# Attention and mixture-of-experts kernel: the router's steps spread over ticks, the second norm's rows and a gate made on ScalarE

## Chip, cores and metric

One core of a Trainium2 chip. The metric is device time in microseconds for one execution of the whole kernel; the number of a kernel is the median of its runs.

## What is computed

For x of shape (8, 512, 128), float32:

```python
x = x + attention(layernorm(x))     # 16 heads of 8 channels, causal, W_qkv, W_proj, biases
x = x + experts(layernorm(x))
# experts(xf), 8 experts, hidden width 512:
logits = xf @ Wg                    # (4096, 8)
top_vals, top_idx = top_k(logits, 2)
gate = softmax(top_vals)
comb = einsum('tke,tk->te', one_hot(top_idx), gate) * alpha
hdn = layernorm(xf) * ln_w[e] + ln_b[e]
y_e = gelu(hdn @ fc1_w[e] + fc1_b[e]) @ fc2_w[e] + fc2_b[e]
out = sum over e of y_e * comb[:, e]
```

The router works on the rows that the second layer norm makes (z below), and the experts' own layer norm on z is folded into a second root (`rstd_two[:, 0]`).

## The kernel before

The program is written without a scheduler: every engine walks one list, `schedule`, and takes from it the stages that it has a handler for, in the list's order. Semaphores join the engines. So what stands ahead of a stage in the list stands ahead of it in an engine's queue.

The attention stage is cut into 8 batches x 4 groups of 4 heads, and a group into 11 units (`UNIT`): four of 512 columns, four of 384, and three with more than one head. Group after group gives 352 units. The list runs in ticks n = 0, 1, 2, ...; in each tick stand `pass1` of unit n, `pass2` of unit n - 24, and, seven ticks later and for some units only, one row of `pv`. A batch is 44 ticks.

- `pass1` (TensorE L648, with a causal matmul L644) makes logits in one of six PSUM slots; VectorE takes the row maximum (L940 for one head, L934 for more), which frees the slot.
- `pass2` (TensorE L665) makes the transposed logits less the maximum in a slot of the same ring; ScalarE takes the exponential (L811), GpSimd cuts the diagonal block (L1252), and TensorE multiplies with v (`pv`, L680).
- `max_parts` (GpSimd L1264, L1267) and `maxT` (TensorE L687, VectorE L948) carry the maxima of a group to the second pass. `pv_out` (ScalarE L816) copies a group's result, which SyncE stores.

Everything else is put at a tick by tables, relative to a batch's first tick. `FRONT`, `APPLY`, `SPLIT` and the two `HALF` tables do so for the next batch's layer norm (`ln_stats` L870, `ln_agg` L877 with the add of epsilon L882, GpSimd's root L1163, `ln_apply` in quarters L893), the projections q, k and v, and the three-part splits of q and k (ScalarE L789, GpSimd L1244), which SyncE stacks. `BACK` holds the way from a batch's attention result to the residual (`o_load` to `proj`, VectorE L953, L958, L964, TensorE L695). `ROUTE` and `DISPATCH` hold the router:

| stage | engine, lines | what it does |
|---|---|---|
| r_stats, r_agg | VectorE L870, L877, L888, L889 | mean and variance, two variances |
| r_root | GpSimd L1184 | the two roots |
| r_z | VectorE L893, L976 | z = (x - mean) * root for four tiles of 128 rows, and a ratio |
| zT, gate | TensorE L602, L707; ScalarE L769; VectorE L980 | transpose and logits of 8 experts |
| r_top | VectorE L987 to L1005 | two largest, their indices, their difference, `pick`, `sel` |
| r_exp | GpSimd L1191 | the second gate as a power of e |
| r_copy | ScalarE L828 | second copy of z |
| r_comb | VectorE L1010 to L1020 | gates, alpha, written into z |
| rank | TensorE L715 to L721; VectorE L1026 to L1034 | place of each token in its expert's list |
| dispatch | GpSimd L1235, eight for a batch | z rows written to their places in DRAM |

One PSUM bank, `misc`, serves all small products; each is read at the start of the next tick, or ahead of the next product (`read_misc`). Within VectorE's steps `link` makes every instruction wait for the one before it:

```python
def link(ins):
    ins.then_inc(s_ln, 1)
    chain[0] += 1
    dve.wait_ge(s_ln, chain[0])
```

After tick 358 come the steps of the first table (`t_count` to `t_row`, VectorE), which lists the expert tiles of the first six batches; tiles 0 and 1 are loaded at tick 366. Steps of batches 6 and 7 that are left over when the attention ends stand between the expert tiles by the dictionary `LATE`. There follow 39 expert tiles (`turn_z`, `fc1`, `fc2`, `turn_y`; TensorE L731, L739, L748, L756, ScalarE L834, L841, VectorE L1120, L1126), the first 17 from the first table, the rest after batch 7 is dispatched. At the end y is read back and summed.

## Time and profile before

| | us |
|---|---|
| median of three runs (lowest to highest) | 540.84 (540.76 to 541.0) |
| span of the profiled execution | 560.3 |
| TensorE, VectorE, ScalarE, GpSimd busy | 473.9, 373.1, 322.9, 366.1 |
| first routing (z of batch 0) to last unit's pv | 112 to 367 |
| expert tiles, first to last of TensorE | 369 to 537 |

The time is measured without the profiler; the profiled execution is a separate one, and of it the span alone, from first to last instruction, is known. It is 19.5 us longer than the median. Differences are read in the trace and set against the median.

### The profile page before, as it was taken

What the parts mean: (1) busy time and instruction counts of PE and PEld (TensorE: products, weight loads), DVE (VectorE), ACT (ScalarE), POOL (GpSimd) and SP (SyncE); (2) the same over time, 40 slices, a digit from 0 to 9 for tenths busy, and PEclk for the clock granted to TensorE, in tenths of its full rate; (3) what the DMA queues carried; (4) which work ended last, traced back from release to release, by engine and by line L of the source; (5) the groups of instructions that cost most, each with busy time, mean ns of one, the idle gap of its engine ahead of it and who ended that gap; (6) DMA issues with size and microseconds to landing.
All of it is one profiled execution on the core that took longest, in us unless ns stands there. A gap on an engine that the chain in (4) does not pass through costs nothing.

```text
span 560.3 us, 11807 instructions
## 1 busy us (share of the span) xinstructions
PE 473.9 (85%) x3296; PEld 277.1 (49%) x3296; DVE 373.1 (67%) x1316; ACT 322.9 (58%) x661; POOL 366.1 (65%) x712
## 2 busy tenths in 40 slices
PE   3379999999999998998898988786992999999930
PEld 1134443543443453443444443364981888888920
DVE  4588878889889889889889997741543521222226
ACT  2137786776676776676676666752550555565610
POOL 5956676586986986987887876955556444445520
PEclk9589999999999999999999999897996899999985
DMA  2323133134233234234224212276642685666439
GB/s 62 93 57 105 65 93 109 58 105 118 68 101 117 78 87 129 73 91 130 75 66 130 71 40 79 79 236 213 219 159 86 213 264 180 216 194 187 154 129 328
DMA packets 52726, 70.83 MB, mean 126 GB/s; under 512 B 11063, under 2 KB 38430, under 8 KB 52662
## 3 DMA queue, kind: packets, MB, share of 16 engines
q1 hardware_dynamic: 47478, 59.19, 34.7%
q0 software_dynamic: 4320, 8.53, 4.5%
q10 hardware_dynamic: 864, 2.36, 1.2%
q8 instruction: 27, 0.44, 0.3%
q14 instruction: 37, 0.30, 0.2%
HBM read 36.49 MB, written 20.94 MB: 102 GB/s over the span
## 4 chain that ended last, share of the span: by engine, by line
PE 51%; DVE 17%; issue 8%; POOL 6%; SPq 5%; DMA 4%; another core or an unknown queue 4%; ACT 3%; ACTq 0%; DVEq 0%; POOLq 0%
PE acc_bank L748 10%; PE slots L739 10%; PE slots L648 7%; PE acc_bank L680 7%; PE slots L665 5%; SPq L496 4%; DVE masked L940 3%; PE misc L616 3%; POOL z_dram L1235 2%; DVE z L893 2%; DVE row_max L934 2%; POOL probs L1252 2%; DMA y_in<-y_dram 2%; PE slots L644 2%
## 5 line engine op out<-in xcount | busy, mean ns | idle before, releaser
L811 ACT ACTIVATE probs<-slots 128x512 f32<-128x512 f32 (+1 forms) x352 | 185.6, 562 | 86.0 <-PE slots L665 79.2
L940 DVE CUSTOM_DVE_ANT_0 masked<-slots,causal_row 128x512 bf16<-128x512 f32 (+1 forms) x256 | 148.9, 614 | 20.8 <-PE slots L648 20.7
L648 PE MATMUL slots<-stack_k,stack_q 125*128 125x256 bf16 (+3 forms) x512 | 128.5, 307 | 19.4 <-DVE row_max L940 7.5
L1252 POOL TENSOR_SCALAR_AFFINE_SELECT probs<-probs 128x128 f32<-128x128 f32 (+2 forms) x352 | 116.1, 350 | 41.3 <-ACT probs L811 37.4
L665 PE MATMUL slots<-stack_q,stack_k 128*128 128x256 bf16 (+3 forms) x512 | 125.6, 301 | 2.9 <-DVE row_max L934 1.5
L1282 POOL DMA_INDIRECT y_dram<-y,z_in x71 | 69.7, 982 | 73.4 <-DVE y L1126 56.8
L841 ACT ACTIVATE hidden<-slots,w_in 128x256 f32<-128x256 f32 (+1 forms) x156 | 63.1, 455 | 82.6 <-PE acc_bank L748 29.2
L680 PE MATMUL acc_bank<-probs,v 128*32 128x512 f32 (+3 forms) x1024 | 95.6, 447 | 3.4 <-POOL probs L1252 2.7
L648 PEld LDWEIGHTS slots<-stack_k,stack_q 125*128 125x128 bf16 x512 | 48.3, 99 | 95.4 <-DVE row_max L940 49.7
L1235 POOL DMA_INDIRECT z_dram<-z,pos x64 | 63.6, 994 | 32.1 <-DVE pos L1034 17.7
L748 PE MATMUL acc_bank<-hidden,w_in 128*128 128x256 f32 (+1 forms) x312 | 73.0, 376 | 7.8 <-issue 4.0
L934 DVE TENSOR_REDUCE row_max<-slots 128x2 f32<-128x512 f32 (+1 forms) x96 | 63.7, 689 | 14.0 <-PE slots L648 13.2
L739 PE MATMUL slots<-hdnT,w_in 128*128 128x256 f32 (+1 forms) x312 | 71.1, 372 | 1.4 <-ACT hdnT L834 0.7
L748 PEld LDWEIGHTS acc_bank<-hidden,w_in 128*128 128x128 f32 x312 | 54.6, 196 | 15.9 <-ACT hidden L841 5.8
L739 PEld LDWEIGHTS slots<-hdnT,w_in 128*128 128x128 f32 x312 | 57.4, 197 | 9.8 <-issue 1.9
L665 PEld LDWEIGHTS slots<-stack_q,stack_k 128*128 128x128 bf16 x512 | 46.0, 98 | 25.7 <-issue 6.5
L1126 DVE TENSOR_TENSOR y<-slots,z_in 128x256 f32<-128x256 f32 (+1 forms) x39 | 15.6, 400 | 54.4 <-issue 33.5
L1120 DVE TENSOR_SCALAR yT<-acc_bank,w_in 128x256 f32<-128x256 f32 (+1 forms) x39 | 17.8, 457 | 49.8 <-PE acc_bank L748 37.4
L680 PEld LDWEIGHTS acc_bank<-probs,v 128*32 128x32 f32 x1024 | 20.4, 108 | 36.9 <-issue 17.2
L644 PE MATMUL slots<-causal,ident_b 128*128 128x256 bf16 (+1 forms) x96 | 30.6, 319 | 0.2 <-DVE row_max L940 0.2
L834 ACT ACTIVATE hdnT<-slots,w_in 128x256 f32<-128x256 f32 (+1 forms) x39 | 21.2, 543 | 2.8 <-PE slots L731 2.8
L756 PE MATMUL slots<-ident,yT 128*128 128x128 f32 x71 | 14.6, 280 | 8.0 <-issue 7.6
(168 smaller groups left out, 523.1 us busy)
## 6 DMA issues: line engine op xcount, KB each, us to landing
w_in<-in_wpack SPq DMA_DIRECT2D x39, 516.0 KB
o_dram<-oT SPq DMA_DIRECT2D x32, 256.0 KB, 2.3
stack_k<-parts SPq DMA_DIRECT2D x95, 64.0 KB
stack_q<-parts SPq DMA_DIRECT2D x93, 64.0 KB
z_in<-z_dram SPq DMA_DIRECT2D x32, 132.0 KB
xt<-in_x SPq DMA_DIRECT2D x8, 256.0 KB, 3.7
onT<-o_dram SPq DMA_DIRECT2D x8, 256.0 KB
o_inv<-inv_dram SPq DMA_DIRECT2D x8, 256.0 KB
```

The lines of the kernel that those rows point to most:

```text
L648: mm = pe.matmul(cols[:, i, :], q[0:K1, hh, blk * P:blk * P + P], k[0:K1, hh, 0:w], start=len(heads) == 1, stop=True, skip_group_check=True)
L665: mm = pe.matmul(cols[:, i, :], k[0:K2, hh, blk * P:blk * P + P], q[0:K2, hh, blk * P:T], start=True, stop=True)
L680: mm = pe.matmul(acc_bank[32 * h:32 * h + 32, row * P:T], v1[:, b % 2, row, HPG * hg + h, :], p, start=(row == 0), stop=(row == PV_ORDER[- ...
L739: pe.matmul(half(slots[:, k, :], i), weights(i)[:, k * P:k * P + P], hdnT[:, i % 2, 0:rows_of(i)], start=True, stop=True)\
L748: mm = pe.matmul(half(acc_bank[:, :], i), weights(i)[:, F + k * C:F + k * C + C], hidden[:, i % 2, k, 0:rows_of(i)], start=k == 0, stop=k ...
L811: act.activation(probs_of(n), columns(n, slot), ACT.Exp, scale=SCALE).then_inc(s_exp, 1)
L841: act.activation(hidden[:, i % 2, k, 0:rows_of(i)], half(slots[:, k, :], i), ACT.Gelu_apprx_tanh, bias=aux(i, 2 + k))\
L934: dve.tensor_reduce(largest, columns(n, slot), AX.X, ALU.max).then_inc(s_max, 1)
L940: dve.tensor_tensor_reduce(out=masked[:, n % MASKED, 0:w], in0=slots[:, slot, 0:w], in1=causal_row[:, T - w:T], scale=1.0, scalar=NEG, op0 ...
L1235: pool.indirect_dma_start(out=z_dram[:, :], out_offset=bass.IndirectOffsetOnAxis(ap=pos[:, b % 2, i:i + 1], axis=0), in_=z[:, b % 2, j, n, ...
L1252: pool.affine_select(out=diag, in_=diag, compare_op=ALU.is_ge, fill=0.0, base=0, pattern=[[0, len(heads)], [1, P]], channel_multiplier=-1) ...
L1282: pool.indirect_dma_start(out=y_dram[:, :], out_offset=bass.IndirectOffsetOnAxis(ap=z_in[:, i % Z_RING, n, ID:ID + 1].bitcast(U32), axis=0 ...
```

## The change

- The linked steps of `r_top`, `r_comb` and `rank` become steps of their own, one or two per tick (`STEPS_OF` lists them). `link` gives way to `step`, which counts, and `stepped`, which waits ahead of the instruction that needs the result. `r_stats` comes in two halves and `r_agg` in two steps.
- For batches 0 to 6 z is made by ScalarE as x * root + shift, a tile of 128 rows (a quarter) per tick. VectorE makes `shift` = -mean * root in a new step `r_shift`. In batch 6 the four quarters stand together. Batch 7 keeps VectorE.
- The second gate is `exp(diff)` on ScalarE for batches 0 to 6. Batch 7 keeps GpSimd.
- Between the request of a root and its use lie more ticks: `ln_agg` at 2, `ln_var` at 3, `APPLY` at 7, 8, 8, 9 for 6; `r_shift` at 111. xnT, q, k and the splits follow two ticks later, the dispatches seven. `base` gets two buffers.

```diff
-FRONT = {"ln_stats": 1, "ln_agg": 3, "xnT": 8, "q": 10, "k": 15, "v": 31}
-APPLY = (6, 6, 6, 6)
-SPLIT = ((11, 12, 16, 18), (17, 18, 26, 29))
+FRONT = {"ln_stats": 1, "ln_agg": 2, "ln_var": 3, "xnT": 10, "q": 12, "k": 17, "v": 31}
+APPLY = (7, 8, 8, 9)
+SPLIT = ((13, 14, 18, 20), (19, 20, 28, 31))
...
-ROUTE = (("r_stats", 102), ("r_agg", 105), ("r_root", 105), ("r_z", 109), ("zT", 112), ("gate", 114), ("r_top", 118),
-         ("r_exp", 119), ("r_copy", 114), ("r_comb", 122), ("rank", 124))
-DISPATCH, DISPATCH_STEP = 123, 3
+ROUTE = (("r_stats", 102, 0), ("r_stats", 103, 1), ("r_agg", 104), ("r_var", 105), ("r_root", 105), ("r_shift", 111),
+         ("r_z", 112, 0), ("r_z", 113, 1), ("r_z", 114, 2), ("r_z", 115, 3), ("zT", 117), ("gate", 119), ("r_copy", 118),
+         ("r_max", 120), ("r_index", 121), ("r_diff", 122), ("r_scaled", 123), ("r_exp", 124), ("r_pick", 124),
+         ("r_sel", 125), ("rank", 126), ("g_sum", 126), ("g_first", 127), ("g_second", 128), ("p_mask", 128),
+         ("g_alpha", 129), ("p_sum", 129), ("g_store", 130), ("p_store", 130))
...
+LAST_ROUTE = (("r_stats", 94), ("r_agg", 95), ("r_root", 97), ("r_shift", 101), ("r_z", 101), ("zT", 109), ("gate", 111), ("r_copy", 111),
+              ("r_top", 115), ("r_exp", 116), ("r_comb", 116), ("rank", 118), ("places", 119))
+DISPATCH, DISPATCH_STEP, LAST_EARLY_STEP = 130, 3, 2
...
+            def make_z(b, n):
+                if b == B - 1:
+                    return
+                if n == 0:
+                    wait(act, s_shift, b + 1)
+                    wait(act, s_disp[b % 2], 16 * 2 * NT * (b // 2))
+                ins = act.activation(z[:, b % 2, 0, n, 0:C], xt[:, NT * b + n, :], ACT.Identity,
+                                     scale=rstd_two[:, 0, n:n + 1], bias=shift[:, n:n + 1])
+                if n == NT - 1:
+                    ins.then_inc(s_z, 1)
+
+            def second_gate(b):
+                if b == B - 1:
+                    return
+                wait(act, s_diff, b + 1)
+                act.activation(second[:, :], diff[:, :], ACT.Exp).then_inc(s_second, 1)
...
+            def step(ins):
+
+                ins.then_inc(s_ln, 1)
+                chain[0] += 1
+
+            def stepped():
+
+                dve.wait_ge(s_ln, chain[0])
...
-            def make_z(b):
+            def find_shift(b):
                 wait(dve, s_rtwo, b + 1)
-                wait(dve, s_disp[b % 2], 16 * 2 * NT * (b // 2))
-                normalise(z[:, b % 2, 0, :, 0:C], xt[:, NT * b:NT * b + NT, :], rstd_two[:, 0, :]).then_inc(s_z, 1)
                 dve.tensor_tensor(ratio[:, :], var_two[:, 0, :], rstd_two[:, 0, :], ALU.mult).then_inc(s_ratio, 1)
+                wait(dve, s_z, b)
+                dve.scalar_tensor_tensor(shift[:, :], mean_var[:, :, 0], -1.0, rstd_two[:, 0, :], ALU.mult, ALU.mult)\
+                   .then_inc(s_shift, 1)
...
-                link(last)
+                step(last)
+
+            def find_index(b):
+                stepped()
                 for n in range(NT):
                     last = dve.max_index(top_at[:, n, :], top[:, n, :], gate_in[:, n, :])
-                link(last)
+                step(last)
```

The order of instructions shows three places. In its rows `stats`, `probs` and the like are the tiles of the text above, and `probs<-slots` is the second pass's exponential.

VectorE, routing of batch 3: from the steps of `r_comb` to the last step of `rank`. Before:

```order
L1010 TENSOR_SCALAR denom<-second 128x4
L1011 RECIPROCAL gates<-denom 128x4
L1012 TENSOR_TENSOR gates<-gates,second 128x4
L1015 TENSOR_TENSOR by_alpha<-pick,alpha_s 128x64
L1018 TENSOR_REDUCE alpha_of<-by_alpha 128x8
L1019 COPY z<-token_ids 128x8
L1020 TENSOR_TENSOR z<-alpha_of,gates 128x8
L940 ISA masked,row_max<-slots,causal_row 128x512
```

The change:

```order
L1073 TENSOR_TENSOR sel<-pick 128x32
L983 ISA masked,row_max<-slots,causal_row 128x384
L983 ISA row_max 128x1
L1077 TENSOR_SCALAR denom<-second 128x4
L1105 TENSOR_TENSOR place_of<-misc,base 128x32
L1107 TENSOR_TENSOR base<-misc,base 128x8
L983 ISA masked,row_max<-slots,causal_row 128x384
L983 ISA row_max 128x1
L1081 RECIPROCAL gates<-denom 128x4
L991 COPY max_rows<-misc 48x128
```

The gates' steps stood in one piece and now have units of the first pass between them; one unit lies between the selection and the reading of `rank`.

ScalarE, the end of the attention with batch 6. Before:

```order
L811 ACTIVATE probs<-slots 128x512 x7
L811 ACTIVATE probs<-slots 128x384 x4
L816 ACTIVATE oT<-acc_bank 128x512
L811 ACTIVATE probs<-slots 128x512
L769 ACTIVATE zT<-misc 128x512
L811 ACTIVATE probs<-slots 128x512 x2
L828 ACTIVATE z<-z 128x4x128
L816 ACTIVATE oT<-acc_bank 128x512
```

The change:

```order
L828 ACTIVATE probs<-slots 128x512 x4
L849 ACTIVATE z<-xt,shift,rstd_two 128x128 x4
L828 ACTIVATE probs<-slots 128x512 x3
L828 ACTIVATE probs<-slots 128x384 x4
L833 ACTIVATE oT<-acc_bank 128x512
L828 ACTIVATE probs<-slots 128x512
L786 ACTIVATE zT<-misc 128x512
L828 ACTIVATE probs<-slots 128x512 x2
L862 ACTIVATE z<-z 128x4x128
L858 ACTIVATE second<-diff 128x4
```

The four quarters stand among the seven exponentials, ten exponentials come behind them, and the gate's exponential stands ahead of the last `oT`.

GpSimd, from the tenth tick or so of a period on. Before:

```order
L1244 TENSOR_TENSOR qk<-qk,parts 128x512
L1235 DMA z_dram<-z,pos 35072x132
L1252 AFFINE_SELECT probs<-probs 128x128 x5
L1184 TENSOR_TENSOR rstd_two<-var_two,minus_half 128x8
L1252 AFFINE_SELECT probs<-probs 128x128
L1244 TENSOR_TENSOR parts<-qk,parts 128x512
L1244 TENSOR_TENSOR qk<-qk,parts 128x512
```

The change:

```order
L1327 DMA z_dram<-z,pos 35072x132
L1344 AFFINE_SELECT probs<-probs 128x128
L1336 TENSOR_TENSOR qk<-qk,parts 128x512
L1344 AFFINE_SELECT probs<-probs 128x128 x2
L1327 DMA z_dram<-z,pos 35072x132
L1344 AFFINE_SELECT probs<-probs 128x128
L1275 TENSOR_TENSOR rstd_two<-var_two,minus_half 128x8
L1344 AFFINE_SELECT probs<-probs 128x128 x2
L1327 DMA z_dram<-z,pos 35072x132
L1344 AFFINE_SELECT probs<-probs 128x128
L1336 TENSOR_TENSOR parts<-qk,parts 128x512
L1336 TENSOR_TENSOR qk<-qk,parts 128x512
```

Between the first split and the last two there was one dispatch; now there are two, and one more just ahead of them.

## Rows read from the trace of the kernel before

**Rows 1.** The page: span, and busy time of each engine (share, instructions)
```profile
span 560.3 us, 11807 instructions
...
PE 473.9 (85%) x3296; PEld 277.1 (49%) x3296; DVE 373.1 (67%) x1316; ACT 322.9 (58%) x661; POOL 366.1 (65%) x712
```

**Rows 2.** Windows of one period: busy us (instructions) of each engine, TensorE's granted clock, DMA
```profile
213.91:217.83 3.92, 3.08 (x25) 0.87 (x25) 3.82 (x19) 2.24 (x5) 1.38 (x3) 1.00 0.46 143
...
221.74:225.66 3.92, 3.52 (x24) 1.10 (x21) 3.88 (x19) 2.47 (x6) 3.09 (x9) 1.00 0.17 50
225.66:229.58 3.92, 2.89 (x30) 1.50 (x29) 3.07 (x12) 1.54 (x4) 3.52 (x9) 1.00 0.31 100
...
241.32:245.24 3.92, 3.53 (x26) 1.40 (x23) 3.92 (x10) 3.04 (x7) 3.77 (x9) 1.00 0.50 151
...
253.07:256.99 3.92, 3.27 (x29) 1.19 (x27) 3.75 (x14) 2.36 (x5) 3.22 (x9) 1.00 0.47 145
sum 43.08, PE 39.77 PEld 18.04 DVE 38.48 ACT 30.04 POOL 34.97; mean PE 3.62 PEld 1.64 DVE 3.50 ACT 2.73 POOL 3.18
```

**Rows 3.** ScalarE in order of time, start and length: the copies of xnT
```profile
62.77 0.60 ACT L769 ACTIVATE xnT<-misc 128x512 f32<-128x512 f32 x1 [0.45 <-PE misc L602]
...
99.69 0.60 ACT L769 ACTIVATE xnT<-misc 128x512 f32<-128x512 f32 x1 [0.45 <-PE misc L602]
...
143.12 0.60 ACT L769 ACTIVATE xnT<-misc 128x512 f32<-128x512 f32 x1 [1.85 <-PE misc L602]
```

**Rows 4.** VectorE in order of time, the same period
```profile
227.29 1.15 DVE L893 TENSOR_SCALAR xn<-xt,mean_var,rstd 128x128 f32<-128x128 f32 x4 [0.85 <-POOL rstd L1163]
...
241.90 2.07 DVE L893 TENSOR_SCALAR z<-xt,mean_var,rstd_two 128x128 f32<-128x128 f32 x4
...
252.99 0.19 DVE L1005 TENSOR_TENSOR sel<-pick 128x32 bf16<-128x32 f32 x1
...
256.35 0.22 DVE L1015 TENSOR_TENSOR by_alpha<-pick,alpha_s 128x64 f32<-128x64 f32 x1
256.60 0.22 DVE L1018 TENSOR_REDUCE alpha_of<-by_alpha 128x8 f32<-128x64 f32 x1
```

**Rows 5.** ScalarE: one group by form; then in order of time, the same period
```profile
L834 ACT ACTIVATE hdnT<-slots,w_in 128x128 f32<-128x128 f32 x7 | 3.3, 469 | 0.0
...
243.93 0.60 ACT L811 ACTIVATE probs<-slots 128x512 f32<-128x512 f32 x1 [0.63 <-PE slots L665]
244.78 0.60 ACT L769 ACTIVATE zT<-misc 128x512 f32<-128x512 f32 x1 [0.25 <-PE misc L602]
245.56 1.16 ACT L811 ACTIVATE probs<-slots 128x512 f32<-128x512 f32 x2 [0.18 <-PE slots L665]
```

**Rows 6.** GpSimd's groups in the period; then GpSimd and TensorE in order of time
```profile
L1235 POOL DMA_INDIRECT z_dram<-z,pos x8 | 8.0, 1000 | 4.2 <-DVE pos L1034 2.5 <-issue 1.1 <-POOL max_parts L1267 0.6
...
L1252 POOL TENSOR_SCALAR_AFFINE_SELECT probs<-probs 128x512 f32<-128x512 f32 x4 | 2.6, 640 | 0.2
L1244 POOL TENSOR_TENSOR qk<-qk,parts 128x512 f32<-128x512 f32 x2 | 2.3, 1152 | 0.0
...
245.67 1.40 POOL L1252 TENSOR_SCALAR_AFFINE_SELECT probs<-probs 128x512 f32<-128x512 f32 x4
...
250.18 0.43 PE L680 MATMUL acc_bank<-probs,v 128*32 128x128 f32 x8
```

**Rows 7.** The tail in order of time: ScalarE, VectorE, GpSimd, TensorE
```profile
354.02 4.47 ACT L811 ACTIVATE probs<-slots 128x512 f32<-128x512 f32 x9
...
362.97 1.08 ACT L811 ACTIVATE probs<-slots 128x512 f32<-128x512 f32 x2
...
359.77 1.44 DVE L893 TENSOR_SCALAR z<-xt,mean_var,rstd_two 128x128 f32<-128x128 f32 x4
...
356.82 1.68 POOL L1184 TENSOR_TENSOR rstd_two<-var_two,minus_half 128x8 f32<-128x8 f32 x1
...
365.76 1.50 PE L680 MATMUL acc_bank<-probs,v 128*32 128x384 f32 x24
```

More of the change, by code:

```diff
@@ L111, in build @@
         n = NG * UNITS * b
-        for name, m in ROUTE:
-            at(n + m - SOONER.get((b, name), 0), name, b)
+        if b < EARLY_BATCHES:
+            for name, m, *part in ROUTE:
+                at(n + m, name, b, *part)
+        else:
+            for name, m in LAST_ROUTE:
+                for step, *part in STEPS_OF.get(name, ((name,),)):
+                    at(n + m, step, b, *part)
         for i in range(2 * NT):
-            at(n + DISPATCH + DISPATCH_STEP * i - SOONER.get((b, "dispatch"), 0), "dispatch", b, i)
+            step = LAST_EARLY_STEP if b == EARLY_BATCHES - 1 else DISPATCH_STEP
+            at(n + DISPATCH + step * i, "dispatch", b, i)
         if b == EARLY_BATCHES - 1:
```

140 lines of the change are left out of this document (90 added, 50 removed).

## The prediction, made before the changed kernel was run

> **What bounds the kernel now.** The page comes first: over the whole span TensorE is busy 85%, VectorE 67%, GpSimd 65%, ScalarE 58% [rows 1]. That is an average of two stages. The change moves work in the first, attention and routing up to about 368 us, so I read that one. The median of the runs is 540.84 us, 19.5 us under the span of the profiled execution (560.3 us); I work out differences on the trace and take them off the median unchanged, since the stage runs at the full granted clock (1.00, the 2.4 GHz level) [rows 2].
>
> Second view: one period of 44 ticks, from the end of one batch's gates to the next, cut into eleven pieces [rows 2]. TensorE is busy 39.77 of 43.08 us, VectorE 38.48. The six pieces that are not shown have TensorE busy for (nearly) all of their time. The five shown have nearly all its idle time: 0.84, 0.40, 1.03, 0.39 and 0.65 us, which is 3.31 together and equals 43.08 - 39.77. So neither engine bounds the period; they take turns. Third view: without routing a period lasts 99.69 - 62.77 = 36.9 us, the first one with routing 143.12 - 99.69 = 43.4 us [rows 3]. Routing and the work that comes with it add 6.5 us, while the idle time above shows that half of this is not TensorE's own work. **The floor of a period is about 39.8 us**, unless TensorE's own work changes, and it does not.
>
> Fourth view: VectorE in order of time at those pieces [rows 4]. The normalisation waits 0.85 us for GpSimd's root and then takes 1.15 us in one stretch; z takes 2.07 us in one stretch; the selection at 252.99 ends a run of linked instructions that stand behind one another, and the gates' steps at 256.35 and 256.60 are part of a second such run. TensorE holds at most a few units ahead, as there are six PSUM slots for both passes, so each such stretch turns into TensorE's idle time.
>
> **What is taken off VectorE.** (1) z, 2.07 us for a batch [rows 4], goes to ScalarE for seven of eight batches. One instruction for the shift comes in; its nearest row is the 0.22 us of a step on 64 columns [rows 4], and I take 0.17. (2) The linked steps. A step behind a link starts 0.25 us after a predecessor that is 0.22 long (256.35 and 256.60) [rows 4]; an unlinked one can start inside the end of the last. About 14 links in a batch, each worth between 0.03 (the gap) and 0.15 us (gap and overlap), give 0.4 to 2.1 us; I take 1.2, as several of the steps now stand next to each other all the same. (3) The wait of 0.85 us for the root [rows 4]: four ticks and more now lie between the request and the first normalised quarter. Together VectorE loses 2.07 - 0.17 + 1.2 + 0.85, about 4 us of 43.
>
> **What of it reaches the end.** Only TensorE's idle time can. From routing: 0.84 (gates and places), 0.39 (z), 0.65 (maximum to selection) [rows 2]. I take 0.65, 0.35 and 0.40, not all, since the same steps remain and the ticks with reduces stay full; 1.4 us for a batch, six batches (0 to 5): 8.4 us. From the layer norm: 0.40 and 1.03 [rows 2]; I take 0.2 and 0.6, because the last quarter of xn now stands one tick before TensorE's transpose where all of it stood two before, in ticks where VectorE's reduces leave no room. 0.8 us in the five loaded periods (batches 3 to 7): 4.0 us. **Gain 12.4 us.** Bounds: nothing, if the spread steps only wait elsewhere, and 6 x 1.88 + 5 x 1.43 = 18.4 us, if all five pieces close.
>
> **What is added.** (a) TensorE's rank now comes one tick after VectorE's selection (before: six ticks, [rows 4] has the selection at 252.99). A unit on VectorE and the selection must fit into a tick that has two short matmuls and a row of pv: I charge 0.2 us, between 0 and 0.8, six times: 1.2 us.
>
> (b) ScalarE. Four quarters at 0.469 us, the row of the same function with scale and bias from tiles and 128 columns [rows 5], 1.9 us a batch. They lie in ticks that have an exponential of 0.60 us each, and there ScalarE was idle 0.63 + 0.25 + 0.18 us [rows 5]. But the copy of zT (0.60) moves out of this stretch, so 1.9 stands against 1.7: cost 0, up to 0.5 a batch if the exponentials come late enough for TensorE to see it; TensorE's second pass may run three units ahead, which covers that much. The gate's exponential is one more small ScalarE instruction in place of GpSimd's 1.0 us. For VectorE's own rate there is a row as well: four took 1.44 us where little else ran [rows 7], so ScalarE is the slower engine for this work. The Trainium skill, ScalarE: Activation LUTs, section "Rules for kernel authors", says to put add and multiply on VectorE, not on ScalarE, as VectorE is faster for them. By that rule the move would be a loss of about 0.4 us a batch; by the rows it is a gain as long as VectorE ends last there. The trace agrees with the rule on speed, and not on which engine should have the work. In the period z took 2.07 us, 0.6 more than in the tail [rows 4, 7]. The Trainium skill, SBUF — State Buffer, section "Who interferes with whom", says that VectorE in a two-port mode and GpSimd fully block one another and that ScalarE waits for neither. By it the 0.6 us would go away with the move; if it were only handed to VectorE's next instruction, my gain of z would be 1.44 and not 2.07. No row of this trace decides that.
>
> (c) GpSimd, the part that I trust least. The dispatches of a batch move by 7 ticks, its splits by 2. From the 10th to the 23rd tick of a period its queue now has four dispatches, three splits, the two-norm root and 14 selects. Before it was two dispatches (the first at the ninth tick). A select takes up to 0.64 us, a dispatch 1.0, a split 1.15, the root 1.68 [rows 6, 7]. Before, the select that the fourth row of pv needs ended at 245.67 + 0.64 = 246.3 us, and TensorE used it at 250.18: 3.9 us to spare [rows 6]. Off come two dispatches (2.0 plus their gaps, 2.3), about 1.0 as twenty ticks each become 0.05 us shorter, and 0.7 because the queue no longer starts on a dispatch one tick earlier. That leaves nothing. I charge 0.5 us of TensorE waiting for GpSimd's selects, between 0 and 1.5, in the four periods with dispatches, splits and root together: 2.0 us.
>
> (d) The tail, batch 6. Its z stands in ScalarE's queue between two exponentials of the second pass. VectorE finds the shift only behind the first table, about where z began before, 359.77 [rows 7]. ScalarE reached this place in its queue before at 354.02 + 4 x 0.53 = 356.1 (three exponentials of 512 columns take 1.6) and went on with exponentials to 358.5. Now it **stands until about 360.1**, then makes four quarters (4 x 0.469 less some overlap, 1.7), then has ten exponentials, oT and zT (twelve at the 4.47 / 9 of the row's run): 361.8 + 6.0 = 367.8, where the last exponential ended at 364.05 before [rows 7]. TensorE had slack behind that: pv, the gate and three more rows of pv ran to 367.3 [rows 7]. With the gate (about 1 us) behind zT at 366.8 and 1.5 us of pv it ends near 369.3: 2.0 us later. GpSimd's root of batch 6 (356.8, [rows 7]) has two more dispatches ahead of it, but idle time further up, so some 1 us later and not last. I charge 2.2 us, between 1 and 4. Everything after (the store of the last heads, the weights of the third tile) follows that end, so it passes in full. The gate's exponential of batch 6 stands ahead of oT's last copy and waits for VectorE; this is in the 4. The stage of the experts keeps its order, cost 0.
>
> **Sum:** 12.4 - 1.2 - 0 - 2.0 - 2.2 = 7.0 us; 540.84 - 7.0 = **533.8 us** (1.3% faster). A measurement can tell some 0.2%, 1.1 us, from no change.
>
> **Rivals.**
>
> *All of TensorE's idle time goes.* For: VectorE has 4 us less to do in a period that misses its floor by 3.3; the period without routing shows what TensorE can do. Against: the new short distances in (a) and to xn. 18.4 - 1 = 17.4 us, 523.4 us; this case covers 523 to 529. Chance 0.17.
>
> *ScalarE takes VectorE's place.* For: 1.9 us more in ticks with 1.06 us idle. The rule on add and multiply above would make it so. Against: three units of lead. Then some 0.9 us a batch come back as waits for the exponentials, 5.4 us, and half of the layer norm's 4.0 goes: 7.0 - 7.4, about no change. It covers 538.5 to 542. Chance 0.12.
>
> *GpSimd becomes the bound, and the kernel is slower.* The place is TensorE's pv at ticks 23 to 30 of periods 3 to 6. The price: two dispatches and the late splits in full, some 3 us in each of four periods (12), with the tail at 4 and 0.5 for each rank (3), against 12.4: 6.6 us slower, 547.4 us. It decides from a wait of 12.4 - 1.2 - 2.2 = 9.0, a quarter of which is 2.25 us a period, on. For: GpSimd's queue is full there by my count. Against: 3.9 us to spare before. Chance 0.13.
>
> *The change does not do what it says.* The order of instructions shows z and the steps moved, so nothing is left for this case.
>
> **How the numbers follow.** My own case, 529 to 538.5 us, has 0.58. Below 525 lie some 0.07, a third of the first rival and a little; above 541 some 0.13. The range is 525 to 541. Faster by over 0.2%: 0.58 + 0.17 + 0.05 of the second rival, 0.80. Within it 0.07, slower 0.13.
>
> **What would show it.** Right: a period near 41.3 us between two transposes of xn, no wait of VectorE for the root, TensorE waiting less than 2 us a period, z quarters near 0.47 us on ScalarE, and in the tail a ScalarE stall of some 4 us before the first z quarter of batch 6. Wrong: periods still at 43 us; waits of pv for selects of over 2 us a period; no stall in the tail, which would put the time 2 us lower; or the stage of the experts, from the first expert tile on, changing its length.

## The result, and the profile after

| | before | after |
|---|---|---|
| median of four runs each, us | 540.92 (540.76 to 541.39) | 554.86 (552.77 to 555.19) |
| span of the profiled execution | 560.3 | 553.1 (its own time 554.9) |
| first matmul of an expert tile | 368.56 | 382.53 |

The changed kernel is **slower by 2.44%**, ratio 1.0244, 95% interval 1.0223 to 1.0264, or 13.9 us. The forecast was 533.8 us, with 525 to 541 as its range: wrong in sign and outside the range.

The two spans cannot be compared with each other. The profiled execution of before has a longer stage of the experts than its timed runs have. The kernel before was timed again on four chips: 540 us on one and 562 to 564 on three, and executions like the latter are 20 us longer behind the first expert tile alone. Ahead of it, two profiles of before agree within 0.7 us (368.56 here, 369.28 below). Of the runs further down, one of e4 (796 us), one of e6 (2499 us) and two of e8 (568 us) fell in a slow state and are left out of the ratios. So I measure each kernel at **the turn**, the start of TensorE's first transpose of an expert tile. First before, then after:

```profile
368.56 0.42 PE L731 MATMUL slots<-ident,z_in 128*128 128x128 f32 x2
```

```profile
382.53 0.42 PE L748 MATMUL slots<-ident,z_in 128*128 128x128 f32 x2
```

The turn is 14.0 us later, which is the whole 13.9 us of the times. The busy time of the engines on the page of after hardly tells of it: VectorE has 15 us less than in [rows 1], ScalarE 6 more.

```profile
span 553.1 us, 11783 instructions
...
PE 467.6 (85%) x3264; PEld 274.7 (50%) x3296; DVE 357.8 (65%) x1296; ACT 329.2 (60%) x696; POOL 361.3 (65%) x705
```

ScalarE of after in order of time, the copies of xnT, against [rows 3]:

```profile
64.80 0.60 ACT L786 ACTIVATE xnT<-misc 128x512 f32<-128x512 f32 x1 [0.28 <-PE misc L619]
...
104.09 0.60 ACT L786 ACTIVATE xnT<-misc 128x512 f32<-128x512 f32 x1 [0.28 <-PE misc L619]
...
148.69 0.60 ACT L786 ACTIVATE xnT<-misc 128x512 f32<-128x512 f32 x1 [0.99 <-PE misc L619]
...
193.53 0.60 ACT L786 ACTIVATE xnT<-misc 128x512 f32<-128x512 f32 x1 [0.60 <-PE misc L619]
...
238.35 0.60 ACT L786 ACTIVATE xnT<-misc 128x512 f32<-128x512 f32 x1 [0.60 <-PE misc L619]
```

A period without routing takes 39.3 us where it took 36.9; nothing of the router runs there, so these 2.4 us are a cost of the front. A full period takes 44.8 us where [rows 2] have 43.08. The window of that full period of after:

```profile
193.53:238.35 44.82, 39.60 (x313) 18.24 (x316) 36.83 (x140) 30.92 (x63) 34.13 (x76) 1.00 0.32 92
```

TensorE's work is as forecast (39.60 after 39.77), VectorE has 1.65 us less, and TensorE is idle for 5.2 us instead of 3.3. What it waited for in that period, from the summary of its waits:

```profile
PE slots L665 <- DVE row_max L983: 1.8, 2, 1.1
PE misc L619 <- DVE xn L936: 0.8, 1, 0.8
PE misc L704 <- ACT qk L795: 0.8, 1, 0.8
PE misc L724 <- ACT v L840: 0.7, 1, 0.7
PE misc L732 <- DVE sel L1073: 0.5, 1, 0.5
PE misc L712 <- ACT qk L795: 0.3, 1, 0.3
```

Three of the six are waits for **the one `misc` bank** behind ScalarE's reading of a projection: maxT (L704) behind k, the gate (L724) behind v, proj (L712) behind q. Over the same kind of period the trace of before has none of them. Each wait also stops VectorE, whose queue has the reader of the product ahead of further maxima. VectorE of after, the gate's reading:

```profile
217.89 0.19 DVE L1033 COPY gate_in<-misc 128x32 f32<-128x32 f32 x1 [2.11 <-PE misc L724]
```

The largest wait, for `row_max`, has this behind it. VectorE, GpSimd and TensorE in order of time:

```profile
206.90 0.69 DVE L983 CUSTOM_DVE_ANT_0 masked<-slots,causal_row 128x512 bf16<-128x512 f32 x1
...
207.51 1.73 DVE L1017 TENSOR_TENSOR ratio<-var_two,rstd_two 128x4 f32<-128x4 f32 x1
209.16 0.42 DVE L1019 SCALAR_TENSOR_TENSOR shift<-mean_var,rstd_two 128x4 f32<-128x4 f32 x1
...
206.93 1.17 POOL L1336 TENSOR_TENSOR parts<-qk,parts 128x512 bf16<-128x512 f32 x1
208.05 1.15 POOL L1336 TENSOR_TENSOR qk<-qk,parts 128x512 f32<-128x512 f32 x1
...
210.25 0.34 PE L665 MATMUL slots<-stack_k,stack_q 125*128 125x384 bf16 x1 [1.14 <-DVE row_max L983]
```

The ratio, four columns wide, takes 1.73 us and ends with GpSimd's pair of splits (208.05 + 1.15 = 209.20).

### The profile page after: what moved, and what is told of

It is laid out like the page before. It is cut to its first block, busy times and chain, and to the rows that moved or that the text cites. A ratio compares the mean times of both kernels' runs of the same rounds, so it can differ in the third digit from the quotient of the medians.

```text
span 553.1 us, 11783 instructions
## 1 busy us (share of the span) xinstructions
PE 467.6 (85%) x3264; PEld 274.7 (50%) x3296; DVE 357.8 (65%) x1296; ACT 329.2 (60%) x696; POOL 361.3 (65%) x705
## 4 chain that ended last, share of the span: by engine, by line
PE 51%; DVE 13%; issue 11%; ACT 9%; POOL 6%; DMA 6%; SPq 3%; ACTq 0%; DVEq 0%; POOLq 0%
PE acc_bank L765 10%; PE slots L756 10%; PE acc_bank L697 7%; PE slots L665 7%; PE slots L682 5%; ACT probs L828 3%; PE misc L633 3%; POOL probs L1344 3%; DVE row_max L977 2%; DMA y_in<-y_dram 2%; DVE masked L983 2%; SPq L513 2%; DVE xn L936 2%; ACT qk L795 2%; POOL z_dram L1327 1%
## 5 line engine op out<-in xcount | busy, mean ns | idle before, releaser
L828 ACT ACTIVATE probs<-slots 128x512 f32<-128x512 f32 (+1 forms) x352 | 183.5, 562 | 84.5 <-PE slots L682 76.9
L983 DVE CUSTOM_DVE_ANT_0 masked<-slots,causal_row 128x512 bf16<-128x512 f32 (+1 forms) x256 | 150.9, 613 | 23.1 <-PE slots L665 22.0
L1344 POOL TENSOR_SCALAR_AFFINE_SELECT probs<-probs 128x128 f32<-128x128 f32 (+2 forms) x352 | 118.3, 350 | 71.7 <-ACT probs L828 66.9
L682 PE MATMUL slots<-stack_q,stack_k 128*128 128x384 bf16 (+3 forms) x507 | 124.8, 302 | 3.0 <-DMA stack_q<-max_rows 2.6
L697 PE MATMUL acc_bank<-probs,v 128*32 128x512 f32 (+3 forms) x1024 | 97.4, 454 | 4.5 <-POOL probs L1344 4.5
L1327 POOL DMA_INDIRECT z_dram<-z,pos x64 | 63.9, 998 | 22.3 <-issue 12.4
L756 PE MATMUL slots<-hdnT,w_in 128*128 128x256 f32 (+1 forms) x312 | 68.5, 362 | 1.4 <-ACT hdnT L868 0.7
L765 PE MATMUL acc_bank<-hidden,w_in 128*128 128x256 f32 (+1 forms) x312 | 68.1, 361 | 0.0
L756 PEld LDWEIGHTS slots<-hdnT,w_in 128*128 128x128 f32 x312 | 55.3, 190 | 8.7 <-issue 1.9
L983 DVE DVE_READ_ACCUMULATOR2_ANT row_max<- 128x1 f32 x256 | 20.8, 81 | 0.0
L661 PE MATMUL slots<-causal,ident_b 128*128 128x256 bf16 (+1 forms) x69 | 20.3, 295 | 0.3 <-DVE row_max L983 0.2
```

The costliest lines, as they stand in the source:

```text
L682: mm = pe.matmul(cols[:, i, :], k[0:K2, hh, blk * P:blk * P + P], q[0:K2, hh, blk * P:T], start=True, stop=True)
L697: mm = pe.matmul(acc_bank[32 * h:32 * h + 32, row * P:T], v1[:, b % 2, row, HPG * hg + h, :], p, start=(row == 0), stop=(row == PV_ORDER[- ...
L756: pe.matmul(half(slots[:, k, :], i), weights(i)[:, k * P:k * P + P], hdnT[:, i % 2, 0:rows_of(i)], start=True, stop=True)\
L765: mm = pe.matmul(half(acc_bank[:, :], i), weights(i)[:, F + k * C:F + k * C + C], hidden[:, i % 2, k, 0:rows_of(i)], start=k == 0, stop=k ...
L828: act.activation(probs_of(n), columns(n, slot), ACT.Exp, scale=SCALE).then_inc(s_exp, 1)
L983: dve.tensor_tensor_reduce(out=masked[:, n % MASKED, 0:w], in0=slots[:, slot, 0:w], in1=causal_row[:, T - w:T], scale=1.0, scalar=NEG, op0 ...
```

## Experiments

| kernel | time, us | before, same chip | ratio (interval) | late period | turn |
|---|---|---|---|---|---|
| e0 | 562.64 | 561.74 | one run | 43.1 | 369.28 |
| e1 | 562.59 | 561.74 | 1.0021 (0.9997, 1.0045) | 43.8 | 374.26 |
| e2 | 579.35 | 561.74 | 1.0289 (1.0254, 1.0324) | 45.7 | 385.16 |
| e3 | 572.90 | 561.74 | 1.0176 (1.0142, 1.0209) | 44.8 | 382.35 |
| e4 | 554.49 | 540.23 | 1.0268 (1.0247, 1.0288) | 44.8 | 381.65 |
| e5 | 552.58 | 540.23 | 1.0234 (1.0217, 1.0251) | 44.6 | 380.03 |
| e6 | 540.58 | 540.23 | 1.0003 (0.9989, 1.0018) | 42.5 | 367.85 |
| e7 | 545.40 | 540.23 | 1.0094 (1.0076, 1.0112) | 43.8 | 373.51 |
| e8 | 564.68 | 562.18 | 1.0012 (0.9984, 1.0040) | 44.9 | 374.56 |
| e9 | 573.23 | 562.18 | 1.0184 (1.0150, 1.0217) | 44.7 | 382.08 |
| e10 | 556.24 | 562.18 | 0.9884 (0.9844, 0.9924) | 42.6 | 367.34 |
| e11 | 560.82 | 562.18 | 0.9977 (0.9951, 1.0003) | 43.1 | 372.80 |
| e12 | 583.73 | 564.18 | 1.0348 (1.0300, 1.0397) | 47.5 | 390.21 |
| e13 | 567.60 | 564.18 | 1.0058 (1.0028, 1.0088) | 43.7 | 376.22 |
| e14 | 570.43 | 564.18 | 1.0104 (1.0052, 1.0156) | 44.6 | 379.76 |
| e15 | 558.17 | 564.18 | 0.9909 (0.9874, 0.9943) | 42.6 | 366.79 |
| e16 | 554.75 | 540.62 | 1.0259 (1.0241, 1.0277) | 44.8 | 381.79 |
| e17 | 546.26 | 540.62 | 1.0107 (1.0089, 1.0125) | 43.1 | 372.99 |

Late period: from the sixth copy of xnT to the seventh (186.21 to 229.29 in before). Where before takes 540 us, time less turn is 171.7 to 172.4 us for before and 171.9 to 173.3 for the others, so the ratio and the turn say the same. Where before takes 562 to 564, time less turn is 193.4 in e0, 193.5 in e12 and 188.0 to 194.2 in the others, so a turn later by 5 us can be hidden there (e1). **I compare turns and periods.** Two profiles of one kernel differ by 0.7 us (before, e0) and 0.9 us (after, e4) at the turn, and by under 0.05 us in a late period; a difference below these says nothing. The 0.9 us lie in the tail, where TensorE's granted clock falls now and then. It falls in single periods of other runs too, and a turn then holds more than the edit: I give the clock where it does.

### Which part costs: the front's tables or the rest

e0 is before again. e1 is the change with the tables of before for the next batch's front (the two stacking tables, `FIRST_HALF` and `SECOND_HALF`, go with them; `ln_agg` and `ln_var` stay at 2 and 3); e2 is before with the new tables.

```diff
-FRONT = {"ln_stats": 1, "ln_agg": 2, "ln_var": 3, "xnT": 10, "q": 12, "k": 17, "v": 31}
-APPLY = (7, 8, 8, 9)
-SPLIT = ((13, 14, 18, 20), (19, 20, 28, 31))
+FRONT = {"ln_stats": 1, "ln_agg": 2, "ln_var": 3, "xnT": 8, "q": 10, "k": 15, "v": 31}
+APPLY = (6, 6, 6, 6)
+SPLIT = ((11, 12, 16, 18), (17, 18, 26, 29))
...
```

> The kernel before, unchanged, for a second profile. The first one's span is 19.5 us longer than its timed runs, while the changed kernel's profiled execution took as long as its timed runs. Theory A (the first profile fell on a disturbed execution, in the stage of the experts): span near 539 us, turn of the first expert tile still at 368 to 369 us, the waits of 6 and 12 us at 376 and 419 us gone. Rival (profiling itself lengthens this kernel): span near 560 us again.

> The change, with the layer norm's, projections' and splits' ticks of before (xnT 8, q 10, k 15, quarters of xn at tick 6, splits as before). Theory 1 (the two ticks' shift puts q one tick ahead of proj, k in one tick with maxT, and the last quarter of xn next to its transpose, all on the one misc bank, so TensorE waits for ScalarE's copy and VectorE): 540 to 545 us, the wait for the copy of qk gone. Theory 2 (ScalarE's z, and VectorE's ratio and shift caught behind GpSimd, cost the time; the shift of the front costs only what is seen before the first routing, 3.7 us): 550 to 552 us.

> The kernel before with nothing but the change's ticks for xnT, q, k, quarters of xn and splits. Theory 1 (shift of the front): 548 us or more, the copy of qk waited for in every period. Theory 2: 543 to 545 us.

e0's profiled execution took 562.64 us on a chip where the timed runs of before took 560.04 to 563.64, so profiling by itself does not lengthen the kernel there.

Measured from the side of the change, the tables cost 382.5 - 374.3 = 8.3 us; put on before, they cost 385.2 - 368.6 = 16.6 us. Of the 16.6, about 1.9 are TensorE's clock: in e2's period without routing (41.49 us long) it is granted 0.96 on average and 0.50 from 98 to 100 us, behind a wait of 2.25 us, and TensorE is busy 38.00 us where before has 36.13. So the front's tables are 8.3 us of the 14.0. The rest of the change costs the other 5.7 us on the old tables, and gives 2.6 us back on the new ones, or some 0.7 without the fall of the clock: the parts collide with each other, and their costs do not add.

### The tail: who makes z of batch 6

e3 is the change with `make_z` on VectorE for batch 6 too (`if b >= 6` for `if b == B - 1`). e4 is the change again, on the chip that e5 to e7 used.

> The change, but z of batch 6 is made by VectorE. Theory 3 (ScalarE's queue stands for the shift of batch 6 behind the table, which costs the tail 2 to 4 us): 551 to 553 us and the first expert tile 2 to 4 us earlier than 382.5. Rival (the tail is set by pv, the gate and GpSimd, and ScalarE has slack there): 554 to 555 us.

> The change, unchanged, beside the kernel before on the same chip as the other runs of this call. If only the chip makes before take 541 or 562 us, the difference stays 13 to 15 us and the first expert tile turns near 382.5 us.

In e3 the turn is at 382.35 after 382.53, no difference. ScalarE of after does stand for the shift, though for a shorter time than the forecast had:

```profile
370.61 1.65 ACT L849 ACTIVATE z<-xt,shift,rstd_two 128x128 f32<-128x128 f32 x4 [2.48 <-DVE shift L1019]
```

Without it the tail is no shorter. From the last `proj` ahead of it to the turn there are 368.56 - 348.78 = 19.8 us in before, 382.53 - 358.51 = 24.0 in after. TensorE's waits from 340 us to the turn name others, first before and then after:

```profile
PE acc_bank L680 <- POOL probs L1252: 2.7, 2, 1.8
PE misc L715 <- DVE sel L1005: 1.1, 1, 1.1
```

```profile
PE acc_bank L697 <- POOL probs L1344: 4.3, 2, 2.4
PE misc L732 <- DVE sel L1073: 2.5, 2, 1.2
```

Together 3.0 us more, of which 1.3 us (one of the two waits for `sel`) lie ahead of the last `proj`. GpSimd of after has eight dispatches from 356.16 to 373.86 with the selects between them. That they cost the 1.6 us of the first row is a reading; no run moved them. The larger part of the 4.2 us is TensorE's clock, as the windows from the last `proj` to the turn show, before and then after:

```profile
348.78:368.56 19.78, 15.07 (x142) 7.27 (x138) 12.54 (x60) 12.13 (x25) 15.16 (x31) 0.91 0.34 112
```

```profile
358.51:382.53 24.02, 17.51 (x140) 7.75 (x138) 11.34 (x60) 13.56 (x30) 18.17 (x35) 0.79 0.31 98
```

TensorE is busy 2.4 us longer for the same work, at a mean granted clock of 0.79 after 0.91; its idle time is 1.8 us more. The clock differs between executions of one kernel: in e4 the same stretch takes 21.9 us at 0.84, so of the 4.2 us 2.1 are gone there.

### The shared bank: k, q and v, one tick apart

```diff
-FRONT = {... "q": 12, "k": 17, "v": 31}
+FRONT = {... "q": 12, "k": 16, "v": 31}   e5
+FRONT = {... "q": 11, "k": 16, "v": 31}   e9
+FRONT = {... "q": 12, "k": 17, "v": 32}   e13
```

> The change with k at tick 16, no longer in one tick with maxT (17). Theory 1a (one bank with two products in one tick is what costs): TensorE's wait for the copy of qk ahead of max_parts (0.8 us a period) goes, seven periods, 5 us or so faster than the change. Theory 1b (the late xn and q beside proj cost it, maxT is hidden): within 1.5 us of the change.

> The change with q at 11 and k at 16: q is no longer one tick ahead of proj (13), k no longer in maxT's tick. Theory 1d: 4 to 6 us faster than the change, 2 to 4 more than k alone gave. Theory 1c: no more than 1 us beyond k alone, which was 1.9 us faster than the change.

> The change with v at 32 alone, out of the gate's tick. With the front's ticks of before this took the period from 43.8 to 42.5 us. Theory 1a: the same here, 1 us or more a period, the first expert tile 5 us or more earlier than 382. Rival (with the late front another wait takes its place): 1 to 2 us in all.

k: the turn comes 2.5 us earlier than in the change (1.6 than in e4), a late period takes 0.25 us less, and maxT's wait over 60 to 340 us falls from 4.7 to 2.7. With q moved as well it is 382.08; what k gave is gone again. The trace of e9 shows where: over the same stretch the wait of proj for q is gone (1.7 us), but q now waits for the copy of xnT one tick ahead of it (1.5 us in all), and the wait for `row_max` grows from 7.3 to 8.8, as the ratio takes 2.04 us in place of 1.72. v: **6.3 us** of 14.0 for one number, 1.17 us a period. That is rather too low, since in e13's period without routing the clock falls to 0.50 from 98 to 100 us, behind a wait of 2.13 us, and the period takes 41.1 us where after has 39.3. The gate's product is at tick 119, and 119 - 2 x 44 = 31, v's own tick; before it was at 114, which is 26. In the period of e13 the row of L724 is gone and the others stand nearly as they were.

### The front back, and v out of the gate's tick

e6 is e1 with v at 32. e7 is e1 with VectorE making z in its quarters, v at 31. e10 is e6 with VectorE making z of batch 6. e15 is e10 with `r_shift` at 109 and the layer norm's first three steps one tick earlier.

> The front's ticks of before, and v at tick 32, one behind the gate (119 is 31 of its period) where both stood in one tick. Theory 1a: the 0.69 us wait of the gate for ScalarE's copy of v goes, and VectorE's 2.1 us idle time with it; six batches, 4 us less than the run with the front's ticks of before alone, so 2 to 4 us faster than before. Rival (VectorE and GpSimd behind it set the period anyway): same as that run, within 1.5 us of before.

> The front's ticks of before, and z on VectorE for all batches, still a quarter per tick; the second gate stays on ScalarE. Theory 4 (ScalarE's z is worth its 2 us of VectorE a batch): slower than the run with the front's ticks of before alone by 4 us or more, less some 3 us for the tail, so 1 to 5 us slower than before. Rival 5 (VectorE had that room once the steps are spread, and ScalarE's late copies of v and zT hold TensorE up): 3 us or more faster than before.

> The front's ticks of before, v at 32, and z of batch 6 on VectorE: the parts of the change that should pay, without the three that should not. The tail gives back 2 to 3 us: 2 to 3 us faster than before. Rival: with batch 6 on VectorE the table's chain and z hold the end up in another way, same as before.

> The front's ticks of before with the layer norm's statistics one tick earlier (0, 1, 2), v at 32, ratio and shift at 109, z of batch 6 on VectorE. Against the run with v and z of batch 6 alone: VectorE's 0.98 us for the root and 1.2 us of ratio go, 0.5 to 1 us a period; 5 us or more faster than before, the first expert tile at 362 to 365 us. Rival (TensorE at its floor of 39.8 and GpSimd now set the period): no more than 1 us beyond that run.

e6 against e1: 374.26 to 367.85, 6.4 us, the same as e13 shows from the other side. With it turn and time are those of before: up to the last copy of xnT e6 is 2.9 us ahead, and the tail takes 2.2 us of it back. Its period and TensorE's waits in it:

```profile
184.18:226.72 42.54, 39.01 (x314) 18.25 (x317) 36.31 (x140) 31.05 (x63) 34.19 (x76) 1.00 0.33 97
```

```profile
PE slots L665 <- DVE row_max L983: 1.0, 2, 0.7
PE misc L619 <- DVE max_rows L991: 0.7, 1, 0.7
PE acc_bank L697 <- POOL probs L1344: 0.5, 1, 0.5
PE misc L704 <- POOL max_parts L1359: 0.5, 1, 0.5
PE misc L732 <- DVE sel L1073: 0.5, 1, 0.5
```

So the spread steps, ScalarE's z and v one tick later are together worth 0.5 us a period (43.1 to 42.5), once nothing collides; the forecast had 1.4 for the routing and 0.8 for the layer norm.

e7 against e1 (both with v at 31) is the comparison for z: 373.51 and 374.26, no difference, both with periods of 43.8 us. VectorE has 37.07 us of work in a period with z and 36.11 without. Neither bounds it: **which engine makes z does not matter here**, while v's tick stands in the way. With v at 32 this pair was not run. e10 and e15 take less time than before where they ran (0.9884 and 0.9909), but only 1.2 and 1.8 us of that is at the turn against 368.56; the other 4 to 5 us lie in the stage of the experts, on chips where that stage takes 20 us longer. Their periods are 0.5 us shorter than those of before, as e6's are, and e6 gained nothing in its time. No run shows what they do on the chip where before takes 540 us. e15 was to come to 362 to 365 us and came to 366.79. Its ratio was to get shorter and takes 2.50 us, where e10's takes 1.22; its late period is 42.58 us all the same, after 42.57. So a longer hold of the ratio need not reach the end.

### What is late by itself: the splits, the quarters of xn

e8 is e6 with the change's ticks for the splits and their stackings; xnT, q, k and xn's quarters stay at the ticks of before. e11 is e6 with `APPLY = (6, 6, 7, 7)`, so xn's last quarter stands one tick ahead of TensorE's transpose, as in the change.

> The run with the front's ticks of before and v at 32, but with the change's later ticks for the splits and their stacking (q and k stay at 10 and 15). Theory 1c (the late splits are the costly part of the front: they meet ScalarE's z quarters, VectorE's ratio behind GpSimd, and SyncE's stores of the maxima queue behind the late stackings): 4 us or more over that run. Theory 1d (the products on the one bank are the costly part): within 2 us of it.

> The run with the front's ticks of before and v at 32, but the last two quarters of xn at tick 7, one tick ahead of the transpose at 8, as the change has it (9 and 10). If this short distance is what TensorE's waits for xn in the change come from (0.5 to 1.2 us a period): 2 to 5 us over that run. If the spreading pays for it (VectorE's wait for the root falls from 0.99 us): within 1 us.

e11: the turn is 4.95 us later, TensorE waits 1.4 us for xn in its late period (first row below), which e6 does not have. About 1 us of the 4.95 is clock: the period ahead of it takes 44.05 us at 0.97 where the late one takes 43.09 at 1.00. e8: 6.7 us later, with the ratio at 3.03 us, VectorE and GpSimd in order of time:

```profile
PE misc L619 <- DVE xn L936: 1.4, 1, 1.4
```

```profile
201.47 3.03 DVE L1017 TENSOR_TENSOR ratio<-var_two,rstd_two 128x4 f32<-128x4 f32 x1
...
202.21 1.16 POOL L1336 TENSOR_TENSOR parts<-qk,parts 128x512 bf16<-128x512 f32 x1
203.32 1.15 POOL L1336 TENSOR_TENSOR qk<-qk,parts 128x512 f32<-128x512 f32 x1
```

201.47 + 3.03 = 204.50, and 203.32 + 1.15 = 204.47: whenever it starts, it ends with the pair. That became the theory of the last runs. e8 holds the comparison within itself. Two of its periods, 44.94 and 44.90 us, have the ratio at 3.03 us, and in both the clock is granted 0.96. In the next period the ratio gets through ahead of the pair, and the period is as long as e6's (42.71), with the splits just as late:

```profile
246.40 0.18 DVE L1017 TENSOR_TENSOR ratio<-var_two,rstd_two 128x4 f32<-128x4 f32 x1
```

```profile
232.55:275.29 42.74, 39.01 (x318) 18.34 (x317) 35.31 (x140) 31.20 (x63) 34.34 (x76) 1.00 0.33 97
```

### The ratio and GpSimd's splits

```diff
-         ... ("r_root", 105), ("r_shift", 111),
+         ... ("r_root", 105), ("r_shift", 109),   e12; e14 with k 16, v 32, VectorE's z in batch 6
+         ... ("r_root", 105), ("r_shift", 112),   e16; e17 with k 16, v 32
```

> The change with the step that makes ratio and shift at tick 109 for 111, ahead of GpSimd's two splits. Theory 1c (ratio, with two inputs in SBUF, stands until GpSimd's splits are through: 1.7 us in the change): ratio takes 0.2 us, TensorE's wait of 1.1 us for the maximum goes, the period falls by about 1 us in four periods, the first expert tile turns 3 to 5 us earlier. Rival (VectorE stands there for something else, or the time goes to the next wait): less than 1 us.

> The change with its late front kept, but k at 16, v at 32, ratio and shift at 109, z of batch 6 on VectorE. If these four and not the late front as such are the loss, all of it goes: 540 us on a chip where before takes 540 (within 3 us of before), the first expert tile near 369. If what is left of the late front (xn next to its transpose, q next to proj) counts: 3 to 7 us slower than before.

> The change, but with r_shift at 112 for 111 (the step stands one unit later in VectorE's queue, still ahead of the first quarter of z). Theory A, the ratio of L1017 is held while GpSimd's two splits run side by side with it: in the change it starts at 207.51, 0.58 us into the pair (206.93 to 209.20), and ends with the pair; put two ticks earlier it started ahead of the pair, took 2.94 us and still ended with it. One tick later it starts at or just behind the end of the pair, so it takes under 0.5 us, TensorE's wait for row_max falls by 0.8 to 1.2 us in each period with routing and splits (four of them), and the expert tiles' first turn moves from 382.5 to 377.5 to 379.5 us. Price: ScalarE gets the shift 0.3 to 0.6 us later, and the transpose of z may wait for it by as much. Rival B, the ratio is slow by itself in this part of the tick (its operands, or VectorE's state behind the masked reduction): it takes 1.3 to 1.7 us again, wherever it stands, and the turn stays within 0.8 us of 382.5.

> The change with three things mended and the front still late: v at 32, k at 16, r_shift at 112. v alone brought the turn from 382.5 to 376.2, k alone to 380.0. If the three collisions are separate and theory A of the run before holds, the turn comes to 376.2 - 2.5 - 4 = about 370 to 372 us, one to three above the kernel before (368.6), and what is left is the last quarter of xn one tick ahead of its transpose and the tail; the time is within 0.6% of the kernel before. Rival: the late front costs by the late splits as such, by what stands behind them in GpSimd's queue and not through the ratio; then the turn stays at 374 us or later, as with the splits alone moved late (374.56).

e12 was to help, and was the slowest of all. The ratio met the pair again, from the front. VectorE, GpSimd and TensorE of e12 in order of time:

```profile
209.04 2.94 DVE L1017 TENSOR_TENSOR ratio<-var_two,rstd_two 128x4 f32<-128x4 f32 x1
...
209.68 1.17 POOL L1336 TENSOR_TENSOR parts<-qk,parts 128x512 bf16<-128x512 f32 x1
210.80 1.15 POOL L1336 TENSOR_TENSOR qk<-qk,parts 128x512 f32<-128x512 f32 x1
...
213.00 0.39 PE L665 MATMUL slots<-stack_k,stack_q 125*128 125x512 bf16 x1 [1.96 <-DVE row_max L983]
```

The wait of 1.96 us in place of 1.14 does not explain 2.7 us a period. Windows of e12 behind it do (the last but two columns are the granted clock, DMA and GB/s):

```profile
208.00:212.00 4.00, 3.02 (x24) 1.29 (x23) 4.00 (x4) 3.04 (x7) 3.63 (x5) 1.00 0.55 148
212.00:214.00 2.00, 1.00 (x4) 0.23 (x4) 2.00 (x6) 0.85 (x2) 1.70 (x7) 1.00 0.46 135
214.00:216.00 2.00, 1.94 (x11) 0.32 (x10) 1.73 (x8) 2.00 (x6) 1.17 (x4) 0.69 0.22 61
216.00:218.00 2.00, 2.00 (x13) 0.50 (x13) 1.10 (x4) 1.35 (x4) 0.58 (x2) 0.50 0.00 0
218.00:220.00 2.00, 2.00 (x25) 1.02 (x25) 0.65 (x3) 1.22 (x4) 1.46 (x2) 0.96 0.12 28
```

Behind the wait TensorE's clock falls to 0.50, the 1.2 GHz level, for about four microseconds: in two such microseconds it gets 13 matmuls done, where the next two hold 25. TensorE is busy 41.4 us in this period of e12 for the same 313 matmuls that took 39.6. One late period of e12 has the same wait and a clock of 1.00, and takes 46.04 us.

e16, one tick the other way, gives the ratio 0.51 us and it ends with the pair once more (209.53 + 0.51 = 210.04; the pair's second starts at 208.85 and takes 1.16):

```profile
209.53 0.51 DVE L1017 TENSOR_TENSOR ratio<-var_two,rstd_two 128x4 f32<-128x4 f32 x1
```

Over 60 to 340 us TensorE's wait for `row_max` falls from 7.3 to 2.7 us, as expected. But the turn moves by 0.7 us instead of 3 to 5, no more than two profiles of the change differ, and the late period not at all. Part of what was freed is spent on two other waits, from the same summary of e16:

```profile
PE misc L724 <- ACT v L840: 4.8, 5, 1.0
...
PE misc L619 <- ACT z L849: 2.1, 5, 0.4
```

The gate's product waits longer for v (4.8 after 3.7), and z's transpose, which never waited, comes up to the quarters (2.1). With v and k out of the way, in e17, the three edits give 1.75 us a period, 44.82 to 43.07, where v alone gave 1.17, k 0.25 and the shift 0.02: some 0.3 us a period that the shift gives only once the other waits are gone. The turn is at 372.99, 9.5 us ahead of the change. The size of the hold itself shows between e14 and e17, which have the same v and k: the ratio is held 2.94 us in e14 and 0.51 in e17, the late periods are 44.6 and 43.1 and the turns 379.76 and 372.99 (e14 also has VectorE's z in batch 6, worth nothing in e3). So rival B falls, theory A was right on the ratio, and wrong on what its first 1.2 us were worth.

What is left from e17 to e6 is 372.99 - 367.85 = 5.1 us. e11 has 4.95 us for the xn quarters alone, on the old tables. The tail is 22.7 us in e17 and 24.0 in e6. The sizes fit, though no run moved the quarters of e17. The 14.0 us then read: 9.5 for v, k and the shift (e17), 5.1 for the rest of the late front (e17 to e6), less 0.7 from e6 to before. e14 keeps the late front and the held ratio and takes 6.3 us more than before on its chip: mending the other collisions does not bring the kernel back.

## Why the prediction was wrong

**The one bank had no line in the sum.** The sum had a gain of 12.4 us and no price for two products of `misc` meeting in one tick. Both terms of the gain failed by it.

"From the layer norm: 0.40 and 1.03 ... 4.0 us" looked at the normalisation alone; "xnT, q, k and the splits follow two ticks later" of the change had no price. The new tables cost 8.3 us (e1). By the runs k with maxT is 1.6 to 2.5 us (e5), xn next to its transpose up to 4.95 (e11), and for q beside proj no run has a price, as e9 trades that wait for another.

"From routing: ... 8.4 us" left out where the gate's product lands. It moved from tick 114 to 119, which is v's tick (31 + 88), and v itself did not move. That costs 6.3 us (e13) or 6.4 (e1 to e6), more than the 5.7 us that the change without the front's tables loses. Without it the spread steps give 0.5 us a late period, not 1.4 for the routing and 0.8 for the layer norm, and the tail takes most of that.

I never laid the ticks of FRONT, GROUP, BACK and ROUTE side by side. Doing so shows gate at 119 and v at 31 + 88, maxT and k at 17, proj behind q.

**xn.** I wrote that the last quarter one tick ahead of the transpose would cost part of the gain. It costs 0.8 us of waiting in the late period of after (4.4 in six periods), and 4.95 us in e11 by itself, about 1 of it clock. The wait for the root did shrink, as forecast (0.38 us at its first quarter at 235.06, 0.85 in [rows 4]), and gave nothing.

**z off VectorE.** Forecast 2.07 us a batch, with the caution that 0.6 of it might be "only handed to VectorE's next instruction". Nearly all of it was: in after ratio and shift take 1.73 + 0.42 = 2.15 us, where z took 2.07 [rows 4] and the ratio behind it 0.35. VectorE's own time fell by 1.65 us a period, and that did not reach the end (e7 against e1).

**(a) rank** one tick behind the selection: forecast 0.2, measured 0.5 us for each batch in after. **(b) ScalarE:** forecast 0.469 us for a quarter, measured 0.48 to 0.50, and cost nothing, as said; the rival that ScalarE takes over is out. **(c) GpSimd's selects**, forecast 2.0 us: in the steady periods pv waits for them 0.2 us in all. The rival on this place named the right engine and the wrong victim. GpSimd's late splits cost time not by its queue but by holding VectorE's ratio: 6.7 us in e8, clock and all, and 0.7 us in the change as it stands (e16). Its 547.4 us was 7.5 us short, and as its mechanism did not occur, its coming out on the right side of no change is luck. **(d) tail:** forecast 2.2, measured 4.2 us (2.1 in e4), of which 2.4 are a clock of 0.79 after 0.91, with the ScalarE stand at 2.48 us instead of 4 and worth nothing (e3).

**Not a failure:** TensorE's own work stayed at its floor (39.6), and the stage of the experts kept its length where before takes 540 us (171.7 to 172.4 and 171.9 to 173.3 us). Of what was to show the forecast right, the short waits for the root and the stand of ScalarE in the tail came; a period of 41.3 us did not.

## What to carry to other kernels

When a table moves a step by one tick, write down for its old and its new tick every step that uses the same single buffer, on all engines and one batch further on; here two products in one tick cost 6 us and one number mended it. When an operation leaves an engine because another engine held it up, look at what takes its place: here the hold passed to the next operation. Read the granted clock beside every difference of two runs: in e2, e8, e11, e12, e13 and the tail a fall of it takes 1 to 2.4 us each time. And test repairs together as well as alone: the shift's tick gave nothing a period by itself and 0.3 us with the two others mended.

## What the runs showed of the hardware

**A VectorE operation of 4 columns takes as long as GpSimd's neighbours let it.** The ratio, with both inputs in SBUF, takes 0.15 to 0.25 us by itself and 0.51, 1.21, 1.73, 2.94 and 3.03 us beside GpSimd's two splits of 1.15 us, ending within 0.1 us of them each time. The Trainium skill, SBUF — State Buffer, section "Who interferes with whom", says that a VectorE instruction with two SBUF inputs contends with a GpSimd instruction that reads SBUF; the trace agrees. The same page of the Trainium skill, section "SBUF: two separate sides", says that whichever of the two starts first gets the port for the whole instruction. In e12 the ratio's record starts at 209.04, 0.64 us ahead of the first split, and still a select of 0.31 us at 209.41 and both splits, all of usual length, pass it. GpSimd was at a dispatch (208.35 to 209.38) when it began. Either the record starts ahead of the grant, or GpSimd keeps the port over operations that follow each other, or the rule has an exception. No run tells which. A dispatch does not always hold it: in e8 the ratio at 246.40 takes 0.18 us inside the dispatch from 245.93 to 246.96.

**The same wait, with and without the clock.** In e12 and e8 waits of 1.96 and 2.45 us are followed by granted clocks of 0.50 and 0.52 (2 us windows). In e14 the same wait at the same place, 1.98 us, is followed by 1.00 all along:

```profile
162.00:164.00 2.00, 0.51 (x2) 0.11 (x2) 2.00 (x7) 0.65 (x2) 1.77 (x7) 1.00 0.62 180
164.00:166.00 2.00, 1.94 (x14) 0.40 (x14) 2.00 (x9) 1.86 (x5) 1.60 (x5) 1.00 0.34 90
166.00:168.00 2.00, 2.00 (x21) 0.88 (x18) 1.39 (x7) 2.00 (x5) 0.59 (x2) 1.00 0.06 15
```

Of e12's four periods with this wait three lost the clock, of e8's three two. In e12 TensorE is busy 41.4 us in a period that lost it and 39.9 in one that did not, in e8 40.6 and 39.0. So a wait near 2 us can cost its own length or some 1.5 us more.

**Chips differ in one stage.** The same program takes 540 us on one chip and 562 to 564 on three others. The difference lies behind the turn: after and e4, which take 554 to 555 us, turn at 382.53 and 381.65, and e3, with the same turn (382.35), takes 572.90 on one of the three, its profile having 189.6 us behind the turn where after has 170.6. Of before there is no profile of an execution of 540 us.
